# 32-column value products in batches, compact row sums and a mask row inside the maximum, in a fused attention and quantised-MLP kernel

## What is computed

```
q = (xn @ Wq) in 16 heads of 32;  k, v = xn @ Wkv in 4 heads of 32, each used by 4 query heads
scores = q k^T / sqrt(32) + slope_h * (s - t), only for s <= t
out    = softmax(scores) v, heads side by side, then @ Wo + bo
gate, up = xn @ Wg^T, xn @ Wu^T     (Wg, Wu, Wd: 4-bit codes times a scale for each 32 values; 4096 rows)
ffn    = (gelu_tanh(gate) * up) @ Wd^T
```

## Time and profile before

| what | value |
|---|---|
| median of 3 runs | 1803.49 us |
| lowest and highest | 1800.28, 1804.3 us |
| the profiled execution's own time | 1803.61 us |
| its span, first to last instruction | 1801.8 us |
| mean granted TensorE clock | 0.987 of full speed |
| busy shares PE, DVE, ACT, POOL | 95%, 79%, 58%, 51% |

### The profile page before, as it was taken

One profiled execution on the slowest core, in us unless ns is written; L12 is line 12 of the kernel. 1 busy time (PEld: TensorE's weight loads), 2 busy tenths in 40 slices (PEclk: granted clock), 3 DMA queues, 4 the chain that ended last, 5 costly groups with the idle time before them and its releaser, 6 DMA issues. The chain is left out here.

```text
span 1801.8 us, 26844 instructions
## 1 busy us (share of the span) xinstructions
PE 1717.2 (95%) x8528; PEld 942.6 (52%) x8528; DVE 1430.1 (79%) x2630; ACT 1044.8 (58%) x1715; POOL 920.7 (51%) x787
## 2 busy tenths in 40 slices
PE   4989999999999999999999999999999999999948
PEld 3764555555555555555555555555555555555536
DVE  6869788787878787887878796877878787878748
ACT  2336657475656667475756566574756565665720
POOL 3315636363645546364646455463646454564627
PEclk9999999999999999999999999999999999999969
DMA  6760020202020210202020201102020202012073
GB/s 188 205 194 15 23 68 16 65 25 66 22 64 15 58 33 19 72 16 66 25 66 20 67 14 45 46 16 71 20 66 25 62 17 73 14 35 56 16 210 130
DMA packets 80747, 104.65 MB, mean 58 GB/s; under 512 B 27056, under 2 KB 46512, under 8 KB 78816
## 3 DMA queue, kind: packets, MB, share of 16 engines
q1 hardware_dynamic: 80608, 102.93, 20.6%
HBM read 68.03 MB, written 22.02 MB: 50 GB/s over the span
## 5 line engine op out<-in xcount | busy, mean ns | idle before, releaser
L1317 POOL TENSOR_TENSOR plo<-p,phi 128x512 f16<-128x512 f32 (+1 forms) x576 | 649.0, 1130 | 409.9 <-ACT phi L1157 408.2
L1150 ACT ACTIVATE p<-score_ps,pshift 128x512 f32<-128x512 f32 (+1 forms) x576 | 380.1, 660 | 317.6 <-DVE score_ps L1237 176.5
L1157 ACT ACTIVATE phi<-p 128x512 f16<-128x512 f32 (+1 forms) x576 | 349.8, 607 | 15.3
L1324 POOL TENSOR_TENSOR il<-prod,ih 128x512 f16<-128x512 f32 x128 | 156.5, 1222 | 330.1 <-DVE ih L1224 330.1
L1082 PE MATMUL score_ps<-qst,kst 128*128 128x512 f32 (+3 forms) x640 | 317.9, 513 | 0.0
L1251 DVE TENSOR_REDUCE mxp<-max_ps 128x1 f32<-128x512 f32 (+2 forms) x320 | 202.1, 631 | 55.1 <-PE max_ps L1057 42.3
L1230 DVE TENSOR_TENSOR acc<-down_ps,acc 128x512 f32<-128x512 f32 x256 | 174.9, 683 | 62.0 <-PE down_ps L1031 61.9
L1098 PE MATMUL o_ps<-plo,vst 128*96 128x512 f16 (+3 forms) x640 | 211.7, 347 | 0.0
L1098 PE MATMUL o_ps<-phi,vst 128*96 128x512 f16 (+3 forms) x640 | 211.6, 347 | 0.0
L1251 DVE TENSOR_REDUCE mxp<-turn_ps 128x1 f32<-128x512 f32 (+3 forms) x320 | 184.8, 577 | 20.1 <-PE turn_ps L1060 8.5
L1044 PE MATMUL gate_ps<-xh,wh 128*128 128x512 f16 x512 | 197.8, 386 | 0.2 <-DVE gl L1208 0.2
(11 more groups left out here) (172 smaller groups left out, 2731.3 us busy)
## 6 DMA issues: line engine op xcount, KB each, us to landing
qst<-q_parts SPq DMA_DIRECT2D x204, 64.0 KB
kst<-k_parts SPq DMA_DIRECT2D x48, 256.0 KB, 4.0
o<-oraw SPq DMA_DIRECT2D x192, 64.0 KB, 2.0
vst<-v_parts SPq DMA_DIRECT2D x17, 512.0 KB, 5.8
q_parts<-o SPq DMA_DIRECT2D x24, 256.0 KB, 3.3
raw<-L_ffn_gate_W_packed_dram SPq DMA_DIRECT2D x18, 256.0 KB, 3.0
raw<-n_L_ffn_up_W_packed_dram SPq DMA_DIRECT2D x18, 256.0 KB, 3.1
raw<-L_ffn_down_W_packed_dram SPq DMA_DIRECT2D x18, 256.0 KB, 4.0
```

Source lines behind the costliest of these rows:

```text
L1150: nc.scalar.activation(p32[n % PR][:, 0:cols], score_ps[:, 0:cols], ACT.Exp, bias=pshift[:, 0:1]).then_inc(exp_done, 1)
L1157: nc.scalar.activation(phi[n % PP][:, 0:cols], p32[n % PR][:, 0:cols], ACT.Copy).then_inc(phi_done, 1)
L1317: nc.gpsimd.tensor_tensor(plo[n % PP][:, 0:cols], p32[n % PR][:, 0:cols], phi[n % PP][:, 0:cols], ALU.subtract).then_inc(plo_done, 1)
L1324: nc.gpsimd.tensor_tensor(il[w % 2][:, a, :], prod[a][:], ih[w % 2][:, a, :], ALU.subtract).then_inc(il_done, 1)
```

## The change

The value products change form. `values` now takes a batch of up to eight blocks of one chunk (batches of 3, 7, 8, 3, 8 and 7 blocks in an iteration, at slots 12, 20, 28, 32, 40 and 47). It multiplies with 32 columns of `vst` at a time and gives each of the array's four column groups its own product: high v by `phi`, low v by `phi`, high v by `plo`, and in the fourth a row sum. The product of low v and `plo`, which came along before, is left out. The remaining row-sum products go to the fourth group and to the first three of a new bank, `l_ps`. Four parts of row sums come out, each in 32 equal rows. One row of each goes through DRAM (`l_s`), is loaded compactly as 128 x 4 x 16, summed and inverted by DVE, written back (`r_s`) and spread over 32 rows as `rb`; POOL adds three value parts in two steps and multiplies by `rb`. `phi` and `plo` become rings of 12; `vst` is held once. The `down` pieces run one wave late, one in every three slots, into one bank, and the last four after the loop. `turn_max` moves half a slot later, and `max_rows` to the end of its slot. The mask matmuls and the separate mask additions on DVE go: a diagonal maximum is one operation that adds a row `mask_row` and takes the maximum.

```diff
-OPARTS = 3
+VPARTS, LPARTS = 3, 4
+O_DMAS = VPARTS + LPARTS
-VALUES_AT = {s + PV_LAG: n for s, n in SCORE_AT.items()}
+BATCHES = [list(range(n, min(n + 8, BLK_END[c]))) for c in range(NCH)
+           for n in range(BLK_END[c - 1] if c else 0, BLK_END[c], 8)]
+VALUES_AT = {SLOT_OF[blocks[-1]] + PV_LAG: b for b, blocks in enumerate(BATCHES)}
-RECIP_AT = {20: 0, 21: 1, 22: 2, 23: 3}
-ADD_PARTS_AT, NORMALISE_AT = 22, 25
+ROW_SUMS_AT = 14
+ADD_PARTS_AT, NORMALISE_AT = (19, 23), 36
@@ ffn_pieces
-            out += [("gate", w, a, 0), ("gate", w, a, 1), ("up", w, a, 0), ("up", w, a, 1)]
-            if w:
-                out += [("down", w - 1, 2 * a, 0), ("down", w - 1, 2 * a + 1, 0)]
-    return out + [("down", NCH - 1, t, 0) for t in range(TPC)]
+            out += [("gate", w, a, 0), ("gate", w, a, 1), ("down", w - 1, 2 * a, 0),
+                    ("up", w, a, 0), ("up", w, a, 1), ("down", w - 1, 2 * a + 1, 0)]
+    return out
@@ output_steps
-        nc.vector.reciprocal(o3[b][:, 1, cols], o3[b][:, 1, cols]).then_inc(recip_done, 1)
+    def load_sums(sp, h):
...
+        sp.dma_start(lp[:], l_s[h % 2].rearrange("q (p f) -> p q f", f=LF)).then_inc(lp_in, 16)
+    def row_sums(dve, h):
...
+        nc.vector.tensor_reduce(lsum[:], lp[:].rearrange("p q f -> p f q"), AX.X, ALU.add).then_inc(lsum_done, 1)
...
+        nc.vector.reciprocal(lrec[:], lsum[:]).then_inc(recip_done, 1)
+    def store_recips(sp, h):
...
+        sp.dma_start(r_s[h % 2].rearrange("(p f) -> p f", f=LF), lrec[:]).then_inc(r_out, 16)
+    def spread_recips(sp, h):
...
+        for c in range(NCH):
+            sp.dma_start(rb[c * HD:(c + 1) * HD, :], r_s[h % 2, c * CH:(c + 1) * CH].rearrange("(o t) -> o t", o=1)
+                         .broadcast_to([HD, CH])).then_inc(rb_in, 16)
@@ main_loop
-        PR, PP = 3, 4
+        PR, PP = 3, 12
@@ sync, gather_o
+                    sp.dma_start(l_s[par, 0:1, cols], oraw[c % 2][VPARTS * HD:VPARTS * HD + 1, :]
+                                 ).then_inc(o_out[c % 2], 16)
+                    for q in range(1, LPARTS):
+                        sp.dma_start(l_s[par, q:q + 1, cols], lraw[(q - 1) * HD:(q - 1) * HD + 1, :]
+                                     ).then_inc(o_out[c % 2], 16)
@@ tensor, maximum
-                        if diag and c < DVE_MASKS_FROM:
-                            mm = nc.tensor.matmul(dst[:, cols - P:cols], identb[:], mask_ts[:], start=False,
-                                                     stop=True, skip_group_check=True)
@@ tensor, values
+                    def product(bank, g, n, src, of, start):
+                        c, tiles, _ = BLOCKS[n]
+                        for j, col, tok in tiles:
+                            mm = nc.tensor.matmul(
+                                bank[g * HD:(g + 1) * HD, tok:CH], vst[:, j, of * HD:(of + 1) * HD],
+                                src[n % PP][:, col:col + CH - tok], start=start, stop=n == BLK_END[c] - 1,
+                                skip_group_check=True)
+                        return mm
...
+                        for k, n in enumerate(blocks):
+                            product(o_ps, 0, n, phi, 0, first and k == 0)
+                            product(o_ps, 1, n, phi, 2, first and k == 0)
+                            mm = product(o_ps, 2, n, plo, 0, first and k == 0)
+                            product(o_ps, 3, *ones[k], 1, first and k == 0)
...
+                        for k in range(count):
+                            g = (k + 3) % 4
+                            mm = product(o_ps if g == 3 else l_ps, g, *ones[count + k], 1,
+                                         first and c > 0 and 0 < k < 4)
@@ tensor, the walk
                         mlp(s, 0)
+                        if s - 1 in TURN_MAX_AT:
+                            turn_max(TURN_MAX_AT[s - 1])
                         if s in VALUES_AT:
...
                         mlp(s, 1)
-                        if s in TURN_MAX_AT:
-                            turn_max(TURN_MAX_AT[s])
@@ scalar, o_copy
-                        nc.scalar.activation(oraw[c % 2][:], o_ps[0:OPARTS * HD, :], ACT.Copy, scale=oback[0:OPARTS * HD, 0:1]
+                        nc.scalar.activation(oraw[c % 2][:], o_ps[:], ACT.Copy, scale=oback[:, 0:1]).then_inc(oraw_done, 1)
+                        if i * NCH + c:
+                            act.wait_ge(o_out[(c + 1) % 2], ((i * NCH + c - 1) // 2 + 1) * 16 * O_DMAS)
+                        nc.scalar.activation(lraw[:], l_ps[0:3 * HD, :], ACT.Copy).then_inc(oraw_done, 1)
@@ vector, reduce
-                            nc.vector.tensor_tensor(own, own, mask_ts[:], ALU.add).then_inc(own_done, 1)
+                        if m == c:
+                            nc.vector.tensor_tensor_reduce(
+                                pair_ps[n % 2][:, 0:cols], pair_ps[n % 2][:, 0:cols], mask_row[:, CH - cols:CH], 1.0, -3e38,
+                                ALU.add, ALU.max, mxp[c % 2][:, t, m:m + 1]).then_inc(red_done, 1)
+                            return
```

More of the change, by code:

```diff
@@ L57 @@
 PV_LAG = 3
-OPARTS = 3
+VPARTS, LPARTS = 3, 4
+O_DMAS = VPARTS + LPARTS
+LF = T // P
 PSHIFT = 15 * math.log(2)
@@ new lines, in add_parts @@
+    def add_parts(pool, h, step):
+        o = o3[h % 2]
+        if step == 0:
+            for out in o_out:
+                pool.wait_ge(out, 16 * O_DMAS * NCH // 2 * (h + 1))
+            if h:
+                pool.wait_ge(on_out, 16 * h)
+            nc.gpsimd.tensor_tensor(on[:], o[:, 0, :], o[:, 1, :], ALU.add).then_inc(osum_done, 1)
+        else:
+            pool.wait_ge(osum_done, 2 * h + 1)
+            nc.gpsimd.tensor_tensor(on[:], on[:], o[:, 2, :], ALU.add).then_inc(osum_done, 1)
@@ L1011, in _, with down @@
                 for b in range(2):
-                    sp.wait_ge(o_out[b], after(16 * OPARTS * HEADS * NCH // 2))
+                    sp.wait_ge(o_out[b], 16 * O_DMAS * HEADS * NCH // 2)
             @block.tensor
             def _(pe):
+                def down(wave, t, half, dst):
+                    g, n = wave // NCH, wave * TPC + t
+                    for q in range(3 * half, 3 * half + 3):
+                        if q == 0:
+                            pe.wait_ge(ih_done, 2 * wave + 2)
+                            if dst is down_ps:
+                                pe.wait_ge(acc_done, after(n))
+                        b, term = q // 3, q % 3
+                        if term == 2:
+                            pe.wait_ge(il_done, after(2 * wave + b + 1))
+                        lhs = (ih, ih, il)[term][wave % 2][:, b, t * P:(t + 1) * P]
+                        rhs = (wh, wl, wh)[term][g % 2][:, 2, b, :]
+                        mm = nc.tensor.matmul(dst[:], lhs, rhs, start=(q == 0), stop=(q == 5))
+                    if half:
+                        mm.then_inc(down_done, 1)
                 def body(i, par, pair):
@@ L1123, in _ @@
                 loop(pe, body)
+                pe.wait_ge(gelu_done, after(HEADS * GU))
+                pe.wait_ge(prod_done, after(HEADS * GU))
+                pe.wait_ge(exp_done, after(HEADS * NBLK))
+                for t in range(TPC):
+                    for half in range(2):
+                        down(HEADS * NCH - 1, t, half, (down_ps, gate_ps, up_ps, score_ps)[t])
             @block.scalar
@@ L1193, in _, with accumulate @@
             def _(dve):
+                def accumulate(n, bank):
+                    dve.wait_ge(down_done, after(n + 1))
+                    dve.wait_ge(acc_done, after(n))
+                    nc.vector.tensor_tensor(acc[:, n % NT, :], bank[:], acc[:, n % NT, :], ALU.add).then_inc(acc_done, 1)
                 def body(i, par, pair):
@@ L1455, in _ @@
             def _(pool):
-                add_parts(pool, HEADS, 1)
-                normalise(pool, HEADS, 1)
+                for step in range(2):
+                    add_parts(pool, HEADS - 1, step)
+                normalise(pool, HEADS - 1)
                 pool.wait_ge(bias_in, 16)
@@ L1471, in _ @@
                                             ).then_inc(diag_done, 1)
-                for q in range(4):
-                    reciprocals(dve, HEADS, q, 1)
                 dve.wait_ge(wo_hi, 1)
```

255 lines of the change are left out of this document (133 added, 122 removed).

## The result

The changed kernel takes 1815.53 us (median of 4 runs, 1814.47 to 1816.3) and the kernel before 1802.34 (4 runs beside it): a ratio of 1.0067, 95% interval [1.0055, 1.0079]. It is slower by 0.7%, where 1762 us, and so a gain of 2.3%, was forecast; the time lies in the stated range, but on the other side of the kernel before. The profiled execution has a span of 1812.7 us, 10.9 more than before.

What follows compares the result with a forecast made beforehand. PE, busy 95% of the span at full clock, was taken to set the time. Terms of -34 - 8 - 18 + 16 + 3 = -41 us against the profiled 1803.6 us gave 1762 us, range 1700 to 1825 us.

Steps and rivals of the forecast that it cites:

- Values, -34: Value products on PE: packed 32-column batches fall from 14.7 to 12.6 us an iteration, -34 us in all.
- the first rival: Value batches on PE: packing as good as on paper, 9.6 us an iteration, 1705 us in all; chance 0.20.
- The slow rival: Value batches on PE: 32-column products do not really overlap, 19.7 us an iteration, 1869 us in all; chance 0.20.
- Masks, -8: 128 mask matmuls leave PE, -8 us; on DVE a pair replaces each masked maximum, PE not waiting for it.
- Turn, -18: Later turn of the maxima: PE's waits for `exp` go, -18 us, with bounds -23 and 0.
- the row, charged with 0.3 us: ACT's copy of the turned maxima for the next scores: up to 0.6 us late, charged 5 us in all.
- What runs out of cover: Shorter PE work hides less of ACT, DVE and chunk loads: +16 us, 1 us an iteration, bounds 0 and 2.5.
- The ends, +3: First iteration and epilogue: less `down` work at the start, extra transfers at the end, together +3 us.
- ACT or DVE becomes the bound: Whole loop: lost cover at its upper bound, +40 instead of +16 us, 1787 us in all; chance 0.15.

Runs made afterwards that it cites:

- b_red: Kernel before, with only the negation of the maxima rewritten as three reductions on DVE; 1781.79 us, ratio 0.9875 to the kernel before.
- l_neg: Changed kernel with its late turn of the maxima kept and the negation moved to GpSimd; 1758.79 us, ratio 0.9746 to the kernel before.
- a_weights: Changed kernel with the turn in its old place, negation on GpSimd and three weight turns moved later; 1734.24 us, ratio 0.9618 to the kernel before.
- a_red: Changed kernel with the turn in its old place and the negation as three reductions on DVE; 1757.14 us, ratio 0.9743 to the kernel before.
- a_down: Changed kernel, turn in its old place, last wave's `down` pieces back in the last four slots over three banks; 1842.88 us, ratio 1.0207 to the kernel before.
- a_turn: Changed kernel with the turn of the maxima and its row copy back in the old places; 1798.3 us, ratio 0.9968 to the kernel before.

## Why the prediction was wrong

- **Values, -34: right mechanism, too dear.** Measured 14.7 - 10.9 = 3.8 us an iteration, -61. I had each two-piece block hold up the groups, 2 us an iteration in all; in the trace a batch with one is only some 0.1 us over an even split of its columns, so in this term the first rival's price was the nearer one. The Trainium skill, "TensorEngine Tiling (Array Packing)", Key Properties, says that a switch of modes drains the engine. The trace agrees in that both ends of a batch cost something: 0.1 us each way, where I had charged 0.163 once. The slow rival (no overlap) falls.
- **Masks, -8: right** in PE's work (0.45 us an iteration), by that estimate; alone the part took 0.36 us off the iteration and brought 4 us. The pair on DVE costs what was forecast, 690 and 142 ns for 512 columns.
- **Turn, -18: wrong.** Alone 6 us, in the changed kernel a loss of 17. I looked at what is late next for PE (the row, charged with 0.3 us) and took ACT to be free. The row waits of 0.6 us each, the bound I had named, are 10.5 us; and the maxima behind the turn waited too.
- **"What runs out of cover", +16: the step that failed.** With the turn's term it stood for all of PE's stalls: together -2 us, where the trace has +74. I compared sums by stretch, DVE 45.5 of 49 us, and called that "close". DVE in fact came to 43.4 us of 53.9, no more than a fair share; what made it late was a chain in slots 6, 14 and 25 in which an operation of 0.17 us takes up to 1.16. The rows were there before the prediction, in the view from which the earlier trace rows are taken, and I read past them:

```profile
L1261 DVE SCALAR_TENSOR_TENSOR nmx<-mxc,nmx 128x4 fp32r<-128x4 f32 x64 | 41.1, 641 | 2.2
L1259 DVE TENSOR_SCALAR nmx<-mxc 128x4 fp32r<-128x4 f32 x64 | 28.0, 438 | 2.2
```

  Against 170 ns for the reduction of the same four numbers, 641 ns should have been a question. It was also what stood behind the wait of the earlier trace rows: `b_red` takes all of it away.

  How much of the growth it is can be estimated from the iterations, with each kernel's better cure. It takes 4.0 us out of the changed kernel as it stands (`l_neg`) and 1.4 out of the kernel before (`b_red`, 98.2 us), so the hold-up accounts for 2.6 of the 4.65 us, 42 of 74 us in all. Once cured, the late turn still costs 0.8 us. Slots 39 and 43, where PE waits for ACT's `exp` (11.5 us in the list above), cost another 0.8, which `a_weights` takes away; a loss of cover of the kind that I had in mind. Some 0.4 us is not accounted for. So about 2 us an iteration, 33 us in all, have nothing to do with the hold-up, where I had charged 16 here and 5 for the row.
- **The ends, +3: +6.** The first iteration gave 5.7 us, not 3 (the second begins at 221.7 in place of 227.4, and 1.5 of that stood ahead of the first MLP matmul). The tail costs 11, not 6: the row sums' load, priced at 2.6 us, is issued at 1735.46 behind the bulk loads of the epilogue, and DVE has it at 1746.34; in the loop it lands in 1.9 us. That the loads ahead of it are the reason was not tested.

```profile
1746.34 0.26 DVE L244 TENSOR_REDUCE lsum<-lp 128x16 f32<-128x64 f32 x1 [17.95 <-DMA lp<-l_parts]
```

Summed: -61 - 7 + 74 + 6 = +12 us, against +10.9 in the spans. Of the rivals, "ACT or DVE becomes the bound" (1787) named the engine but not the mechanism, and stopped at +40.

**Open:** why the late turn still costs 0.8 us an iteration once cured, with no wait in the list (l_neg, 0.2 to 0.5 us at each of three turns); whether slots 39 and 43 were ACT's queue alone, since `a_weights` moved DVE's rounding of those weights along with ACT's, and DVE's decoding of the weights beside them is longer than its shortest too (`wf<-dec,sc`, 0.68 to 1.65 us in `a_red`, mean 1.08), which no run changed; and the packing without late `down` matmuls, since `a_down` added waits and falls of the clock of its own.

## What to carry to other kernels

Before an engine's slack is read from sums, look for groups whose mean is several times that of their like in size: an operation on four numbers that takes 0.6 us on the average is being held up, and the hold-up is paid by whatever is queued behind it. A speed-up of the bounding engine removes the slack that paid for such things; find them first, and cure them first, since here the cure was worth more than the change (41 us against 25). On VectorE beside a busy GpSimd, write small SBUF-to-SBUF steps as reductions, or give them to GpSimd itself where its queue is short.

## What the runs showed of the hardware

- Four 32-column products on four column groups start mostly 3 to 4 ns apart (records around 700.2 us of `a_turn`: 700.206, .209, .213, .216) and sustain a round of four 512-column products every 0.216 us, at full granted clock: four times the rate of one at a time.
- Entering and leaving such a batch costs about 0.1 us each (0.309 us from start to start on the way in, 0.312 on the way out behind a 512-column product, where 0.216 is usual).
- An operation on 4 elements a partition took from 0.16 to 1.16 us on DVE beside POOL's subtraction; written as a reduction it took 0.16 each time, also in the middle of 3.39 us of POOL's work. The operations held up ended together with POOL's, all 63 in the changed kernel.
- A wait of 1.9 us on PE near the end of an iteration of `a_down` was followed in 11 of 16 cases by 3.4 us at 1.2 GHz, which cost 1.7 us; in the other 5 the clock stayed at 2.4.
